# Both halves of the first layer's value products side by side on TensorE, in a two-layer graph attention kernel

## What is computed

```
# layer 0: softmax over all nodes, values chosen by relation r = adj
q, k = heads(x @ Wq + bq), heads(x @ Wk + bk)
attn = softmax(q @ k.T / sqrt(32))
out  = sum over r of (attn * (adj == r)) @ heads(x @ Wv[r] + bv[r])
x1 = layernorm(x + out @ Wo + bo)
x2 = layernorm(x1 + gelu(x1 @ W1 + b1) @ W2 + b2)
# layer 1: leaky scores, masked softmax
e = leaky(heads(x2 @ Wq') @ heads(x2 @ Wk').T)
h = layernorm(softmax(where(adj > 0, e, -9e15)) @ heads(x2 @ Wv'))
y = layernorm(concat(h, x2) @ Wffn.T) + x2
```

## Time and profile before

| | |
|---|---|
| median of 3 runs | 3207.07 us (3203.78 to 3213.83) |
| profiled execution | 3206.77 us, span 3204.5 us, mean granted TensorE clock 0.988 |
| TensorE (matmul) busy | 3100.9 us, 97% of the span |
| VectorE | 2602.0 us, 81% |
| ScalarE | 2057.2 us, 64% |
| GpSimd | 1433.0 us, 45% |
| DMA | 292.76 MB, mean 91 GB/s |

### The profile page before, as it was taken

How to read it: one execution, slowest core, us unless ns; L and a number is a source line. 1 busy time by engine, 2 the same in 40 slices (tenths; PEclk the granted TensorE clock), 3 DMA queues, 4 the chain that set the end, 5 groups by cost and what they waited for, 6 DMA issues and landing times.

```text
span 3204.5 us, 76322 instructions
## 1 busy us (share of the span) xinstructions
PE 3100.9 (97%) x28139; PEld 2711.9 (85%) x28328; DVE 2602.0 (81%) x4896; ACT 2057.2 (64%) x4303; POOL 1433.0 (45%) x1549
## 2 busy tenths in 40 slices
PE   4899999999999999999999999999999999999996
PEld 3788888888888888888888888888888888888885
DVE  3687888888888888888888888888888888888884
ACT  2566666666666666666666666666666666666664
POOL 1344454454454454454454454454454454454441
PEclk7999999999999999999999999999999999999998
DMA  4333433433433433433433433433433433433431
GB/s 110 83 80 90 105 85 89 105 86 89 104 86 89 105 86 89 105 86 89 105 86 89 104 86 89 105 86 89 103 87 89 103 87 89 104 87 89 103 84 31
DMA packets 218074, 292.76 MB, mean 91 GB/s; under 512 B 31796, under 2 KB 119479, under 8 KB 218039
## 3 DMA queue, kind: packets, MB, share of 16 engines
q1 hardware_dynamic: 218038, 292.30, 39.0%
HBM read 73.02 MB, written 16.78 MB: 28 GB/s over the span
## 4 chain that ended last, share of the span: by engine, by line
PE 88%; issue 4%; ACT 3%; DVE 2%; SPq 1%; DMA 1%; POOL 1%; POOLq 0%; DVEq 0%; ACTq 0%
PE pair L982 49%; PE pair L1012 15%; PE pair L1036 7%; PE pair L1026 6%; PE pair L1091 4%; PE pair L1100 2%; PE pair L1028 2%; ACT probs L560 2%; PE pair L1000 2%; SPq L298 1%; PE pair L987 1%; PE pair L1107 0%; POOL act_r_lo L417 0%; ACT leaky_s L539 0%; DMA stack_a<-qk 0%
## 5 line engine op out<-in xcount | busy, mean ns | idle before, releaser
L417 POOL TENSOR_TENSOR act_r_lo<-act,act_r_hi 128x512 fp32r<-128x512 f32 x256 | 335.8, 1321 | 741.1 <-DVE act_r_hi L946 538.7
L539 ACT ACTIVATE leaky_s<-leaky_s,low_r 128x256 f32<-128x256 f32 x1024 | 506.2, 499 | 2.8 <-DVE low_r L788 2.0
L423 POOL TENSOR_TENSOR probs<-probs,rel 128x512 f32<-128x512 f32 x256 | 293.7, 1170 | 211.4 <-ACT probs L560 123.4
L560 ACT ACTIVATE probs<-pair 128x1024 f32<-128x1024 f32 x256 | 256.9, 1030 | 199.0 <-PE pair L1100 199.0
L792 DVE TENSOR_REDUCE mx_a<-pair 128x4 f32<-128x1024 f32 x256 | 307.7, 1223 | 78.3 <-PE pair L1091 78.1
L533 ACT ACTIVATE leaky_s<-pair 128x1024 f32<-128x1024 f32 x256 | 262.7, 1026 | 159.5 <-PE pair L1028 159.5
L784 DVE TENSOR_TENSOR leaky_s<-pair,leaky_s 128x1024 f32<-128x1024 f32 x256 | 312.3, 1220 | 38.6 <-ACT leaky_s L533 38.4
L788 DVE TENSOR_REDUCE low_r<-leaky_s 128x4 f32<-128x1024 f32 x256 | 310.8, 1214 | 2.2
L529 ACT ACTIVATE probs<-pair 128x1024 f32<-128x1024 f32 x256 | 262.1, 1024 | 65.7 <-PE pair L1036 61.5
L423 POOL TENSOR_TENSOR leaky_s<-probs,rel 128x512 f32<-128x512 f32 x256 | 291.1, 1171 | 0.3 <-ACT probs L560 0.3
L1036 PE MATMUL pair<-ident,leaky_s 128*128 128x128 f32 x2048 | 269.3, 275 | 7.5 <-ACT leaky_s L539 6.6
(11 more groups left out here) (193 smaller groups left out, 8830.1 us busy)
## 6 DMA issues: line engine op xcount, KB each, us to landing
stack_a<-qk SPq DMA_DIRECT2D x768, 128.0 KB, 2.4
stack_r<-qk SPq DMA_DIRECT2D x768, 128.0 KB, 2.4
xt<-in_xT SPq DMA_DIRECT2D x64, 256.0 KB, 3.5
adj_a<-in_adjT SPq DMA_DIRECT2D x64, 256.0 KB, 3.0
xn<-in_x SPq DMA_DIRECT2D x64, 256.0 KB, 3.4
adj_q<-in_adj SPq DMA_DIRECT2D x64, 256.0 KB, 2.9
out<-n SPq DMA_DIRECT2D x64, 256.0 KB, 2.8
probs<-in_w SPq DMA_DIRECT2D x4, 512.0 KB, 4.6
```

Of the source, the lines that this page charges most:

```text
L417: return nc.gpsimd.tensor_tensor(dst, src, hi, ALU.subtract)
L423: last = nc.gpsimd.tensor_tensor(masked_p[g][:, h], probs[:, g, h], rel1[:], ALU.mult)
L539: last = nc.scalar.activation(leaky_s[:, p % SLOTS, k, t], leaky_s[:, p % SLOTS, k, t], ACT.Exp, bias=low_r[:, p, k, t:t + 1], accum_out=d ...
L560: return nc.scalar.activation(probs[:, g, 2 * q:2 * q + 2], pair[b][:], ACT.Exp, scale=SCALE)
```

## The change

`both(0)` and its wait for the second exponential move from behind the third `score_cols` to a place directly ahead of `both(1)`, behind the fourth `score_cols`, `lq`, `lk` and the turned norm. The wait on `heads_r` is left out. Nothing else changes, on TensorE or elsewhere.

```diff
                 if g3 is not None:
                     pe.wait_ge(probs_a.sem, probs_a.at(g3, 1))
                     score_cols(2, B_AC[2]).then_inc(sta_mm.sem, 1)
-                    pe.wait_ge(probs_a.sem, probs_a.at(g3, 2))
-                    if ran(g3, 2):
-                        pe.wait_ge(heads_r.sem, heads_r.at(g3 - 2))
-                    both(0).then_inc(pva_mm.sem, 1)
                     if ran(g3, 1):
                         pe.wait_ge(x2t_split.sem, x2t_split.at(g3 - 1))
                     score_cols(3, B_AC[3]).then_inc(sta_mm.sem, 1)
...
                     pe.wait_ge(ln_done[LN_H].sem, ln_done[LN_H].at(g1))
                     transposed(B_N1T, n1).then_inc(n1t_mm.sem, 1)
                 if g3 is not None:
+                    pe.wait_ge(probs_a.sem, probs_a.at(g3, 2))
+                    both(0).then_inc(pva_mm.sem, 1)
                     pe.wait_ge(probs_a.sem, probs_a.at(g3))
                     both(1).then_inc(pva_mm.sem, 1)
                 if g1 is not None:
```

## The result

The changed kernel takes 3346.26 us (median; 3342.69 to 3351.85) against 3208.35 us of the kernel before: a ratio of 1.0431, 95% interval 1.0416 to 1.0447. It is slower by 138 us. The forecast was slower, with 3287 and a range up to 3316; the time lies 30 us above that range.

What follows compares the result with a forecast made beforehand. TensorE was taken to bound the kernel, so new idle time ahead of the fourth scores adds to the span: +1.30 us in 61 turns plus 1 for two early ones, 80 us on 3207, gives 3287; range 3268 to 3316.

Steps and rivals of the forecast that it cites:

- What bounds the kernel: TensorE sets the pace, with about 0.2 us idle per turn; every new idle microsecond is added to the span.
- (a) The hole: Behind the third scores TensorE waits for `x2t_lo`; the fourth start 2.40 us after the third, against 2.78 before.
- (b): `both(0)` ahead of `both(1)` doesn't pay the 0.09 us more of its second part, so it costs 1.78 us.
- (c): At the fourth scores, the 0.10 us lost when 128-column products follow 32-column ones goes.
- The sum: From the third scores to the first product behind `both(1)`: 9.92 us against 8.62, +1.30 a turn.
- the likeliest case: TensorE's new idle time costs 1.30 us in 61 turns, plus 1, with no clock loss: 3287 us, chance 0.80.
- (d): Later waits, of the query products, the turned norm and `both(0)`, are all met when TensorE comes to them.
- The signs: `x2t_lo` wait about 1.7 us, some 61 times; turn 49.4; TensorE 96 to 97% busy; wrong if half clock in middle.
- rival (1): Idle time ahead of the fourth scores brings the clock down; in half of the turns 48 us more, 3335; chance 0.10.
- The range: 3268 to 3316 us for the whole kernel; what lies outside was given under 0.2.

Runs made afterwards that it cites:

- ten matmuls of fill: Changed kernel with half of the fourth column scores computed five extra times between the third scores and the `x2t_lo` wait; 3279.31 us, ratio 1.0235.
- The two halves apart: Changed kernel with `both(0)` placed directly behind the fourth column scores, ahead of the query and key products; 3396.08 us, ratio 1.0594.
- four matmuls of fill: Changed kernel with four matmuls of the fourth column scores done again between the third scores and the `x2t_lo` wait; 3278.17 us, ratio 1.0230.
- The fill runs: Changed kernel with ten, four or one matmuls of the fourth column scores done again ahead of the `x2t_lo` wait; 3279.31, 3278.17, 3319.21 us.
- one matmul of fill: Changed kernel with a single matmul (0.12 us) of the fourth column scores done again ahead of the `x2t_lo` wait; 3319.21 us, ratio 1.0349.

## Why the prediction was wrong

Point by point, by its own steps.

*What bounds the kernel*: right. What the order took from TensorE went into the span, turn by turn.

*(a) The hole*: right in mechanism and size. The fourth scores start 2.41 after the third, 2.40 was predicted; the list of waits has 103.0 us over 63, where about 100 over 61 were.

*(b) and (c)*: `both(0)` costs 1.75 in its new place (1730.07 to 1731.82), 1.78 was put down, and `both(1)` 1.84. The fourth scores keep their 0.58 to the next start, though nothing of another shape precedes them: the 0.10 that (c) took off wasn't saved there. It seems that a first instruction after a stall pays as one after a crossing does. The third scores point the same way: they begin 0.05 after the exponential that they wait for ends (1514.52 + 1.03 = 1515.55, one exponential taking 1.03, and 1515.60 in the earlier trace rows), nothing of another shape precedes them, and with ten matmuls of fill they take 0.58 to the next start too (1694.60 to 1695.18). No run separates the two causes. The two halves apart cost 0.41 a turn more than together (49.74 against 49.33), so crossings between shapes do have a price; that most of it lay under the idle time ahead of `both(0)` in the kernel before is my reading, not shown.

*The sum*: 9.99 was measured for the stretch (9.92 predicted), +1.37 over 8.62. The next stretch gave 0.10 back: from the first product behind `both(1)` to the masked products 4.08 before (1524.22 to 1528.30) and 3.98 after (1733.66 to 1737.64), probably because stacked rows now arrive with time to spare. The turn is 1.25 longer; 1.30 was predicted. With the clock held, as by four matmuls of fill, the kernel takes 3278 where the likeliest case said 3287: the sum alone was some 9 us too high.

*(d)*: right, no further wait of any size appeared.

*The signs*: the wait, its count and TensorE's 96.7% in the middle came as described, and 49.4 us a turn where the clock holds (49.33). The sign of being wrong that came true is half clock in the middle.

*The step that failed* is the chance given to rival (1), in these words: "The new hole stands with those that did no harm, but close to the border." The likeliest case rested on it, with 0.80 against 0.10, and its sum put the clock at nothing; it cost 1.48 us in 45 of 56 turns. The mechanism was named and nearly priced (3335, by 30 turns at 1.6; 45 of the middle 56 at 1.48 came), and that the price came so near is in part luck, as "half of the turns" stood on no row. Its chance was read from single events. Two waits in the trace of before, 1.64 and 1.75, had left the clock up, and I took that as saying what such a wait does. The changed kernel shows that the same wait does both: a fall follows the 1.66 ahead of 1675.26 and none the 1.67 ahead of 1726.08. At 1.55 it is 24 of 56. A wait that passes once has been seen once; the loop asks the question 61 times. The fill runs show that this was all of the error and more, since adding work to the hole takes 67 us away again, and the rest of the sum was 9 too high. The Trainium skill (TensorE: Matmul & The Clock Gate, A second HAM failure mode) says of another kernel that short idle times between groups of matmuls, coming often enough, make the clock swing between its levels. The trace agrees for holes of 1.67 and 1.55 us in every turn, and not for those of 1.43 and less, which came as often and left the clock up in all 56 turns; with a hole so near the lengths in doubt, it should have raised the chance.

*The range*, up to 3316, took in only the nearer end of rival (1) and left its own figure of 3335 outside; a mechanism whose price is as large as the forecast and whose border is that near belongs inside it.

## What to carry to other kernels

A block between two waits on a saturated engine may be there as cover: before moving it, subtract it from the timeline and see when the next wait ends. If a new idle time of TensorE comes back in every turn, price it twice, by its length and by the clock, and let one wait of nearly that length in the old trace count for little. If the clock falls, a few harmless matmuls in the hole are a remedy to try: here four of them, 0.47 us of work, brought back 68. And where a block waits for a bank or a tile that only half of it touches, issue the other half first: here that was worth 14 us before the change and 81 after it.

## What the runs showed of the hardware that I had not expected

For a hole that comes once a turn in this loop the border is a slope, and a steep one: 0, 24 and 45 long turns of 56 for idle times of 1.43, 1.55 and 1.67 us. The long turns don't fall at random either. They come in runs, three in a row in the kernel with one matmul of fill, and mostly four with one short turn between them in the changed kernel; lengths of consecutive turns there, in us, from the middle:

```
50.84 50.81 50.83 50.82 49.27 50.80 50.86 50.75 50.87 49.35 50.80 50.78 50.75 50.80 49.35
```

The granted clock in the trace says more of that rhythm. Inside a run of long turns one fall of the clock starts 51.20 us after the last, whether the turn takes 50.81 us (the changed kernel) or 51.38 (the halves apart). So the fall comes 0.39 later in each turn of the one and 0.18 earlier in each of the other. Two turns of the changed kernel, with third scores at 1571.22 and 1622.04, have it 3.05 and 3.43 behind these; the clock stands third from the end:

```profile
1574.07:1574.27 0.20, 0.20 (x4) 0.20 (x3) 0.20 (x2) 0.00 (x0) 0.20 (x1) 0.99 0.00 0
1574.27:1574.47 0.20, 0.20 (x3) 0.20 (x3) 0.20 (x2) 0.07 (x1) 0.20 (x1) 0.50 0.00 0
1625.27:1625.47 0.20, 0.20 (x4) 0.20 (x3) 0.20 (x2) 0.20 (x1) 0.20 (x1) 0.99 0.00 0
1625.47:1625.67 0.20, 0.20 (x3) 0.20 (x2) 0.20 (x2) 0.20 (x1) 0.19 (x1) 0.50 0.00 0
```

All falls of the middle start 2.6 to 4.1 us behind the third scores in the changed kernel, 2.5 to 4.0 with the halves apart, and 2.9 to 3.9 with one matmul of fill; a run ends where the next one would lie outside. So the falls keep a beat that isn't the program's, and it seems that the same wait brings the clock down or not by where it stands against that beat, with less room for it when the wait is shorter. This is read from three traces; no run moved a hole against the beat to test it.

And the stretch at the lower level costs more where it meets the 32-column products (3.48 us for 32 of them, 1.87 at full clock) than where it meets query and key products.
